# A graph network of five edge passes on one core: every chunk of edges gathered by GpSimd, none fetched row by row by SP and ACT

## The reference

```python
x = layernorm(x + gin(x))      # segment_sum(x[src], dst); elu(. @ W1 + b1) @ W2 + b2
x = layernorm(x + mpnn(x, e))  # relu([x[src], x[dst], e] @ W1 + b1) @ W2, segment_sum, then an MLP
x = layernorm(x + sage(x))     # mean of x[src] -> h, batch norm, relu, mean of h[src] -> l2norm
x = layernorm(x + rgcn(x, t))  # segment_sum(x[src] @ weight[type], dst)
```

## Time and profile before

| | us |
|---|---|
| median of 3 runs | 9605.86 (9603.74 to 9610.63) |
| the profiled execution's own time | 9613.65 |
| its span, first to last instruction | 9611.7 |
| POOL busy | 7166.3 (75%) |
| PE busy | 4955.0 (52%) |
| PEld busy | 4259.7 (44%) |
| DVE busy | 2604.7 (27%) |
| ACT busy | 1301.8 (14%) |

### The profile page before, as it was taken

The page is one execution under the profiler, slowest core; times in us unless marked ns, Lnnn a source line. Parts: engine busy times, 40 slices in busy tenths (PEclk is TensorE's granted clock), DMA queues, the critical chain, the costliest instruction groups (busy, mean ns, idle before and its releaser), DMA issues.

```text
span 9611.7 us, 127811 instructions
## 1 busy us (share of the span) xinstructions
PE 4955.0 (52%) x23790; PEld 4259.7 (44%) x23791; DVE 2604.7 (27%) x6055; ACT 1301.8 (14%) x2785; POOL 7166.3 (75%) x7594
## 2 busy tenths in 40 slices
PE   4555555566666666344444445666666633333333
PEld 3444444456666665333333334555555522222222
DVE  2222222234444444111121223333333311111111
ACT  1111111111111111000000002222222200000000
POOL 7777777777777777777777777777777667777777
PEclk7555555577777777555555555555555555555555
DMA  3111111133333333111111112222232211111111
GB/s 76 34 34 34 35 34 35 34 93 96 95 94 96 95 95 92 29 31 32 31 32 32 31 31 72 82 83 81 80 84 80 76 32 30 30 30 30 30 30 29
DMA packets 460729, 529.13 MB, mean 55 GB/s; under 512 B 220578, under 2 KB 287616, under 8 KB 459848
## 3 DMA queue, kind: packets, MB, share of 16 engines
q0 software_dynamic: 242880, 349.17, 16.2%
q1 hardware_dynamic: 93785, 88.18, 3.3%
q10 hardware_dynamic: 123247, 83.52, 3.0%
HBM read 442.93 MB, written 77.29 MB: 54 GB/s over the span
## 4 chain that ended last, share of the span: by engine, by line
POOL 70%; issue 23%; PE 3%; ACTq 2%; ACT 1%; DVE 1%; SPq 0%; DMA 0%; POOLq 0%; DVEq 0%
POOL G L520 70%; PE PH L1282 1%; PE PAG L1282 1%; ACTq L383 1%; ACTq L391 1%; PE NA L1282 0%; SPq L422 0%; ACT G L755 0%; PE NB L1282 0%; DVE G L1153 0%; ACT STG L680 0%; ACT Y L663 0%; ACT XT L590 0%; DMA rel_tab<-STG 0%; DVE Y L1038 0%
## 5 line engine op out<-in xcount | busy, mean ns | idle before, releaser
L1282 PE MATMUL PAG<-OH,G 128*64 128x96 f32 (+2 forms) x12126 | 2294.9, 382 | 3742.0 <-DMA G<-rel_tab,IDX 988.0
L1282 PEld LDWEIGHTS PAG<-OH,G 128*64 128x64 f32 (+2 forms) x12126 | 2097.5, 253 | 3971.2 <-issue 3425.2
L520 POOL DMA_INDIRECT G<-rel_tab,IDX x1507 | 1421.9, 944 | 515.7 <-issue 459.6
L520 POOL DMA_INDIRECT G<-far_tab,SRC x1527 | 1440.8, 944 | 485.3 <-issue 465.5
L520 POOL DMA_INDIRECT G<-h_tab,SRC x1524 | 1439.4, 944 | 480.7 <-issue 463.5
L520 POOL DMA_INDIRECT G<-in_x,SRC x1525 | 1440.6, 945 | 475.2 <-issue 464.6
L520 POOL DMA_INDIRECT G<-x_tab,SRC x1507 | 1423.4, 945 | 477.1 <-issue 459.7
L941 DVE TENSOR_TENSOR AGG<-AGG,PAG 64x96 f32 (+2 forms) x980 | 245.8, 251 | 5434.9 <-PE PAG L1282 5432.6
L905 DVE TENSOR_TENSOR OH<-CONST,DREL 128x768 f32<-128x768 f32 x980 | 926.9, 946 | 3.2 <-issue 2.3
L1282 PE MATMUL PAG<-OH,HT 128*128 128x96 f32 x3126 | 615.7, 378 | 583.2 <-ACT HT L748 579.0
L1282 PEld LDWEIGHTS PAG<-OH,HT 128*128 128x128 f32 x3126 | 572.8, 283 | 630.3 <-ACT HT L748 625.3
(11 more groups left out here) (173 smaller groups left out, 3896.4 us busy)
## 6 DMA issues: line engine op xcount, KB each, us to landing
GROWS<-x_tab SPq DMA_DIRECT2D x4096, 0.2 KB
GROWS<-rel_tab SPq DMA_DIRECT2D x4096, 0.2 KB
GROWS<-in_x SPq DMA_DIRECT2D x3584, 0.2 KB
GROWS<-h_tab SPq DMA_DIRECT2D x3456, 0.5 KB
rel_tab<-STG ACTq DMA_DIRECT2D x200, 250.0 KB
GROWS<-far_tab SPq DMA_DIRECT2D x3072, 0.5 KB
GROWS<-x_tab ACTq DMA_DIRECT2D x3072, 0.2 KB
GROWS<-rel_tab ACTq DMA_DIRECT2D x3072, 0.2 KB
```

Source lines behind the costliest of these rows:

```text
L520: pool.indirect_dma_start(out=G[:, h, j, 0:tabs[p].shape[1]], out_offset=None, in_=tabs[p], in_offset=bass.IndirectOffsetOnAxis(ap=numbers ...
L1282: return nc.tensor.matmul(dst, lhsT, rhs, start=start, stop=stop, skip_group_check=True)
```

## The change

All row-by-row fetches go: `GROWS`, the row semaphores, the tables of byte offsets and the two loads and five table steps that made them, `some_rows` on SP and on ACT, and the branches that used them in DVE, ACT and PE. POOL gathers every filled chunk of every super in all five passes, with no branch on `REGULAR_I`. In pass 3 DVE shifts super s's rows ahead of the add of super s - 1, and PE gets an explicit wait for that add. For the relation maps the weights are loaded twice (partitions 0 to 63 and 64 to 127), the flip puts the unit's two halves on the two halves of the partitions, the copy to `XT` is 125 columns wide on 128 partitions and no longer 250 on 64, and the maps are issued as pairs that use different row halves of PE and different `PH` banks; ACT copies and stores them in the order of the pairs.

```diff
-def gnn_kernel(nc, x, xT, src_c, src_e, dst_c, dst_r, type_c, type_e, efT, ...
+def gnn_kernel(nc, x, xT, src_c, dst_c, dst_r, type_c, efT, ...
...
-            (IDX3[:, :], type_c), (SRC_E[:, :], src_e), (IDX3_E[:, :], type_e),
+            (IDX3[:, :], type_c),
...
-(wl2[:, :], Wl2), (wr2[:, :], Wr2), (wrel[:, :], Wrel),
+(wl2[:, :], Wl2), (wr2[:, :], Wr2), (wrel[0:D, :], Wrel), (wrel[D:2 * D, :], Wrel),
...
@@ sync
-                some_rows(0, 0, P * len(SP_SUPERS[0]))
...
-                    if (s + 1) * piece <= P * len(SP_SUPERS[1]):
-                        some_rows(1, s * piece, (s + 1) * piece)
-                for p in range(2, LAYERS):
-                    sp.wait_ge(stored[p - 1], all_stored(p - 1))
-                    some_rows(p, 0, P * len(SP_SUPERS[p]))
@@ gpsimd
-                filled = GROUP - 1 if s in by_rows else filled_chunks(s)
+                filled = filled_chunks(s)
...
-            pool.wait_ge(prep, TABLES_READY)
-            regular = is_regular(pool)
-            with pool.If(regular > 0):
-                layers([set(by_sp) | set(by_act) for by_sp, by_act in zip(SP_SUPERS, ACT_SUPERS)])
-            with pool.If(regular < 1):
-                layers([()] * LAYERS)
@@ scalar
-                    flip_copy(3, u)
+                    act.wait_ge(flipped[3], u + 1)
+                    nc.scalar.activation(XT[:, 0:HALF], PT[:, 0:HALF], ACT.Copy).then_inc(flip_copied[3], 1)
...
-                        a, b = k // 2, k % 2
+                        a, b = k % 2, k // 2
...
-                        some_rows(p, s, registers, starts)
@@ vector
+                        if p == 3:
+                            shift(p, s // SLOTS, h, chunks)
                         if s:
                             add_straight(p, s - 1, starts[s - 1], m)
...
-                        if p == 3:
-                            shift_straight(s, h)
@@ tensor
                 elif p == 3:
                     pe.wait_ge(bn_relu, s + 1)
+                    pe.wait_ge(added, SUPERS * p + s + 2)
...
-                    flip(3, XS, D)
+                    for a in range(2):
+                        last = mm(PT[a * D:(a + 1) * D, 0:HALF], XS[0:HALF, a, :], IDENT[0:HALF, 0:HALF])
+                    last.then_inc(flipped[3], 1)
                     pe.wait_ge(flip_copied[3], u + 1)
-                    for k in range(4):
-                        c = slice(k % 2 * 512, k % 2 * 512 + 512)
-                        mm(PH[k // 2][0:HALF, c], XT[0:D, half(k // 2)], wrel[:, c]).then_inc(l3_map, 1)
+                    for b in range(2):
+                        c = slice(b * 512, b * 512 + 512)
+                        for a in range(2):
+                            k = slice(a * D, (a + 1) * D)
+                            mm(PH[a][0:HALF, c], XT[k, 0:HALF], wrel[k, c]).then_inc(l3_map, 1)
```

More of the change, by code:

```diff
@@ L27 @@
 I16 = mybir.dt.int16
-U8 = mybir.dt.uint8
 ACT = mybir.ActivationFunctionType
@@ L86, in filled_chunks, with gnn_kernel @@
     return max(1, min(GROUP, FILLED - s * GROUP))
[L89 to L101, removed]
+def gnn_kernel(nc, x, xT, src_c, dst_c, dst_r, type_c, efT, W1, b1, W2, b2, mW1, mb1, mW2T, mb2,
                uW1, ub1, uW2, ub2, Wl1, Wr1, sb1, gamma, beta, Wl2, Wr2, sb2, Wrel, out):
@@ L368, in first_left @@
             return eng.value_load(DONE_I[0:1, TURNS:TURNS + 1], min_val=0, max_val=UNITS)
[L370 to L401, removed]
         STORE = [16, 16, 16, 64, 16]
@@ L450, in _ @@
             sp.reg_mov(more, 0)
+            sp.wait_ge(rows_out, ROWS_OUT)
             sp.wait_ge(prep, TABLES_READY)
-            starts = []
-            def some_rows(p, lo, hi):
-                for at in range(lo, hi):
-                    k, e = at // P, at % P
-                    if e == 0 and k >= ROW_BUFS:
-                        row_buffer_free(sp, p, SP_SUPERS[p][k - ROW_BUFS])
-                    if at % AT_ONCE == 0:
-                        starts[:] = row_starts(sp, row_registers, p, SP_SUPERS[p][k] // 2, e)
-                    row(sp, p, k % ROW_BUFS, e, starts[at % AT_ONCE])
+            sp.wait_ge(stored[0], all_stored(0))
             def stream_straight(s, w0):
@@ L508, in _, with gathers @@
         def _(pool):
-            def gathers(p, s, by_rows=()):
+            tabs = [x, far_tab, x2_tab, h_tab, rel_tab]
+            def gathers(p, s):
                 numbers = IDX3 if p == 4 else SRC
@@ L750, in straight @@
                             act.wait_ge(bn_shifted, s + 1)
-                            b, landed = row_buffer(3, s)
-                            if b is not None:
-                                chunks = GROUP - 1
-                                nc.scalar.activation(GROWS[:, b, :], GROWS[:, b, :], ACT.Relu)
-                            nc.scalar.activation(G[:, h, 0:chunks, :], G[:, h, 0:chunks, :], ACT.Relu)\
-                              .then_inc(bn_relu, 1)
+                            rows_ = G[:, h, 0:chunks, :]
+                            nc.scalar.activation(rows_, rows_, ACT.Relu).then_inc(bn_relu, 1)
                         for u, stage in SCHEDULE[s]:
@@ L1315, in _, with sum_window @@
                 pe.reg_mov(reg, 0)
-            def sum_window(p, h, m, by_rows=None, chunks=GROUP):
+            def sum_window(p, h, m, chunks=GROUP):
                 msg = HID[:, h % 2, :].rearrange("p (j c) -> p j c", j=GROUP) if p == 1 else G[:, h, :, :]
                 for j in range(chunks):
-                    rows_ = msg[:, j, 0:m]
-                    if j == GROUP - 1 and by_rows is not None:
-                        rows_ = GROWS[:, by_rows, 0:m]
-                    last = mm(PAG[0:m, 0:WIN], rows_, OH[:, h % 2, j, :], j == 0, j == chunks - 1)
+                    last = mm(PAG[0:m, 0:WIN], msg[:, j, 0:m], OH[:, h % 2, j, :], j == 0, j == chunks - 1)
                 return last
@@ L1381, in sum_straight @@
                     pe.wait_ge(gathered[h], slot_gathered(p, s // SLOTS))
-                b, landed = (None, None) if p == 1 else row_buffer(p, s)
-                if b is not None and p != 3:
-                    pe.wait_ge(row_in[p][b], landed)
-                sum_window(p, h, m, b, filled_chunks(s)).then_inc(summed, 1)
+                sum_window(p, h, m, filled_chunks(s)).then_inc(summed, 1)
             def pre_straight(t):
```

117 lines of the change are left out of this document (28 added, 89 removed).

## The result

| | before | after |
|---|---|---|
| median of the runs on one chip, us | 9607.27 (9603.74 to 9610.63, 4 runs) | 9857.31 (9855.90 to 9858.55, 4 runs) |
| the profiled execution's own time, us | 9613.65 | 9857.38 |
| its span, us | 9611.7 | 9855.6 |
| gathers on POOL | 7590 | 7815 |

The ratio is 1.026, with a 95% interval of 1.0242 to 1.0278: 2.6% slower. The spans differ by 243.9 us. I call this chip A. Four chips stand in this text, and the sign is not the same on all of them; that comes with the experiments.

A forecast was written before the change was run, and what follows sets the result against it. POOL's issue of gathers, 1.249 us each, was taken as the bound. 9613.65 + 281.0 - 18.7 - 2.4 = 9873.6, less 7.8 for the profiled execution's excess over the median: 9866 us, 2.7% slower, range 9850 to 9890.

The forecast's parts named there:

- 225 gathers at 1.249 us, +281.0: POOL, all passes: the row path's 225 chunks return as gathers at 1.249 us each, +281.0 us, all on the path.
- Gather price unchanged: POOL's gathers: no cheaper without row DMAs, taken as 0; bounds -16 and +2 us.
- Rival 3: POOL's gathers: row DMAs slow every gather, so the change is faster, 9397 at 60 ns; 0.02 together with 4 and 5.
- The wait behind pass 3, 37.4: POOL's wait at pass 3's end: 12.3 us to the last add plus 25.1 second part, for 56.1 before; -18.7 us.
- The start at 0, bounds -2 and +4: Kernel start, where POOL waits 8.3 us: two loads fewer and one larger change nothing; 0, bounds -2 and +4 us.
- Slot waits -2.4: POOL's waits for a free slot: those other than the first go with pass 3's backlog, -2.4 us.
- Ends of passes 0 to 2 at 0: Ends of passes 0 to 2, and the tail: no row work in them, so 0; bounds -2 and +2 us.
- 1 (backlog stays, 56 us): Pass 3: add behind shift stretches the consumer loop, pass 3 stays late and its end at 56 us; 9887 us; chance 0.08.
- 2 (pairs don't overlap): Relation maps on PE: paired matmuls don't run in parallel, 3.6 us at unit 48; 9870 us; chance 0.09.
- 4: Gathers: paced by transfers all queues share, not by POOL's issue, so no added time; 9585 us; 0.02 with 3 and 5.
- 5: Row path: never taken, so the change adds no gathers; 9585 us; 0.02 together with 3 and 4.
- 6: Pass 3: a new wait for slots, each 1 us a unit being 50 us; 9916 us; chance 0.03.

The follow-up runs named there:

- the gathers alone: Kernel before with POOL gathering all 7815 chunks while SP and ACT still fetch the rows (rows fetched and gathered): 14331.5 us on chip B, ratio 1.0208.
- fixed rows: Kernel before with POOL gathering every chunk and row DMAs reading fixed addresses, without address loads or register moves: 9891.8 us on chip D, ratio 1.0277.
- the rows alone taken out: Changed kernel with the order of shift and add and the maps both put back as before: 11458.7 us on chip B.
- maps unpaired: Changed kernel with the relation maps put back one after another on one row half, from an `XT` of 64 partitions: 11449.6 us on chip B.
- add first: Changed kernel with pass 3's old order put back, the add of super s - 1 ahead of the shift of super s: 11444.1 us on chip B.
- the kernel with additions: Kernel before with POOL gathering every chunk and register additions in place of each register move and row DMA: 9887.1 us on chip D, ratio 1.0272.

## Why the prediction was right on chip A, and where its steps were off

The forecast was 9866 us; the time was 9857.3, in the range and on the side forecast. In own times of the profiled executions the sum said 9873.6 and the trace 9857.4, 16.2 us less: the four misses below (3.1, 4.3, 8.3 and 2.1), less 1.6, of which 1.5 is the usual gap of 0.3 us that stays where each of the five slot waits was. I had taken 7.8 us off because the profiled execution before was that much above its median; that after is at its median, so the correction hid half of the error, by luck.

- **225 gathers at 1.249 us, +281.0: right.** The pace, with the 11 gaps that go by another name, is 1.2484 us for 1.2488, and 7815 x 1.2484 - 7590 x 1.2488 is about +278. On chip B the gathers alone cost 283 (beside POOL's waits there); on D the two kernels that gather all and keep half of the row path took 261 and 266 more, with the backlog's relief in it. Gathers alone were not run on A.
- **Gather price unchanged: right** within the bounds; 0.4 ns less a gather, -3.1 us. Rival 3, row DMAs that slow every gather, is out on A and also on B and C: 943 to 948 ns, and gaps of 305 to 308 ns where POOL doesn't wait.
- **The wait behind pass 3, 37.4: 33.1.** The backlog went. The count for unit 48 was 12.3 and is 10.0: it used 3.73 us for the sum behind the maps and 1.5 for the last one, and they take 2.86 and 1.02. The granted clock behind the paired block, from the sum of 194 to the last add, in two rows, and then before:

```profile
7864.50:7867.30 2.80, 2.80 (x17) 2.63 (x16) 0.00 (x0) 1.68 (x4) 0.00 (x0) 0.69 0.32 91
7867.30:7871.00 3.70, 2.56 (x15) 2.05 (x15) 0.51 (x2) 1.27 (x5) 0.00 (x0) 0.82 0.32 122
```

```profile
7686.20:7694.00 7.80, 7.34 (x30) 6.63 (x30) 0.97 (x3) 2.04 (x6) 0.00 (x0) 0.50 0.29 93
```

  It is 0.69 and 0.82, where it was 0.50 (1.2 GHz), so part of these sums ran at 2.4 GHz; that is where most of the 2.3 us come from. That the pairs raised the clock is not shown: on D a block of unpaired maps began at 0.97 (7882.50 to 7884.00 us, fixed rows) and took 5.84 us for 7.19. By the timeline the maps end 4.1 us behind the last gather (forecast 4.4), the sum of 194 at 6.9 (8.2) and the last sum starts at 8.6 (10.4). The second part was sized at 25.1 and is 23.1: I held that issuing the last store earlier buys nothing, and the pairs do buy 1.5 us there, and 0.5 in the copies ahead of the maps. That the stores are held by their own engines was right; splitting them gives 3.6 us at once.
- **How the backlog went.** I gave the row work on ACT, the moved shift and the maps as reasons. The kernel with fixed rows keeps the row DMAs, the late shift and the single maps and has, on D, a lag of 14.5 for the 31.0 on A. So on chips like these most of it is POOL's own slower supply, 39 gathers or 49 us more in the pass, with ACT's address loads, which that kernel also lacks, not separated from it. Between 15.9 and 14.5 on D and the 10.0 of the changed kernel on A lie shift ahead, pairs and the rest of the row work. On B, where every lag is longer, the rows fetched and gathered have 30.9 and the rows alone taken out 27.0, so there the order and the pairs bring most of the 11 us.
- **The start at 0, bounds -2 and +4: wrong, -8.3 us.** This step failed. I priced the two loads by their number and didn't look at what stood behind them in SP's queue. The before trace had it: 23.74 us of SP at the weight load behind the two (the row is shown above). The row of the last landing that I used was the consequence.
- **Slot waits -2.4: right,** but for the usual gaps in them. **Ends of passes 0 to 2 at 0:** -2.1 behind pass 2, just outside the bound of 2.
- **Rivals.** 1 (backlog stays, 56 us) is out with 33.1. 2 (pairs don't overlap) is out: 3.78 us for 7.18 at the same clock. 4 and 5 are out with 7815 gathers at the old price. 6 is out: no slot wait longer than 0.3 us.

On chip C the same change is 18.6% faster, and the kernels near it say the same of B. No rival had that: 3 gives faster, but through the gathers' pace, which stays. What changes there is that POOL isn't the bound. The forecast rests on POOL's having no waits, and that is a fact of the chip that the trace came from.

## What to carry to other kernels

Count what the bounding engine issues, times its pace: that term, 281 us, came out at 278 and is all of the loss; the rest gave back 34. Then read the issuing queue behind each DMA that a change takes away, not only the DMA, and read the pass end as two parts, lag and dependent tail. And before taking off work that "lies beside" on SP or ACT as free, or adding it, time both kernels on a second chip: here the kernel with 225 chunks of each run fetched by other engines is 2.5% faster on chip A and takes 23% longer on chip C, and kernels near it say the same of D and B.

## What the runs showed of the hardware

- Two fp32 matmuls of 64 rows on different row halves, into different banks, overlap: 3.78 us for the block of eight at a granted clock of 0.50, 7.18 one after another at 0.50. Blocks that take less, 3.36 us in pairs or 5.84 unpaired, have matmuls in them of 0.59 to 0.66 us for 1.05.
- Stores of 125 partitions keep a share of 0.32 of the engines busy; as 112 and 13 the share is 0.42, and the reader behind the last one starts 2.3 us after its issue and not 7.8, 3.6 us sooner in all. With two loads of 122 partitions SP stood 23 to 24 us at the next DMA; with 128 it passed that DMA in 0.48 us and stood 10.4 us later on, as without them.
- A gather takes 944 ns in some executions and 946 or 947 in others. On B two kernels without row fetches, maps unpaired and add first, whose gathers are the same, differ:

```profile
L447 POOL DMA_INDIRECT G<-h_tab,SRC x1563 | 1475.2, 944 | 774.6 <-issue 447.6 <-remote 210.3 <-PE PAG L1149 95.4
```

```profile
L447 POOL DMA_INDIRECT G<-h_tab,SRC x1563 | 1478.2, 946 | 769.4 <-issue 448.0 <-remote 294.0 <-DMA h_tab<-STG 21.2
```

  Over 7815 gathers that is some 20 us. What decides it is not shown. On D the kernel with additions took 9869 us in one execution, that of the trace, with 944 ns, and 9886 to 9889 in the other three, which fits an execution of the quicker kind among three of the slower; so single times that differ by 0.2% say little here.
- Chips of one kind differ: the kernel before takes 9607 and 9626 us on two, 14,049 and 14,137 on two others, with register moves of up to 1.4 us on the latter (B and C, with row fetches) and 38 ns at most on A. What holds their engines up was not found.
